# Two kinds of expert layer: gate weights spread over 128 rows, the gate's steps in other slots, first products ahead of the first gate weights

## The reference, cut to what matters

```
nx = rmsnorm(X) * g2                                   # per token, 128 values
rw = softmax(nx @ Wr.T + expert_bias)                  # 8 experts
topw, topi = top_k(rw, 2);  topw = softmax(topw)
combine = sum(one_hot(topi, 8) * topw)                 # 8 gate weights a token, 6 are zero
shared = (silu(xf @ sW1.T) * (xf @ sW3.T)) @ sW2.T     # for every token
eo[e]  = (silu(xf @ eW1[e].T) * (xf @ eW3[e].T)) @ eW2[e].T
X + shared + sum over e of combine[:, e] * eo[e]
```

## Time and profile before

| | us |
|---|---|
| median of 3 runs | 3324.93 (3316.59 to 3332.51) |
| the profiled execution, its own time | 3329.29 |
| its span in the profile | 3327.4 |
| mean granted TensorE clock | 0.904 of full speed |
| PE busy | 2785.1 (84%) |
| DVE busy | 2147.6 (65%) |
| POOL busy | 1693.1 (51%) |
| ACT busy | 1467.9 (44%) |

### The profile page before, as it was taken

How to read it: one execution, slowest core, us unless ns; L and a number is a source line. 1 busy time by engine, 2 the same in 40 slices (tenths; PEclk the granted TensorE clock), 3 DMA queues, 4 the chain that set the end, 5 groups by cost and what they waited for, 6 DMA issues and landing times. The chain is left out here.

```text
span 3327.4 us, 45520 instructions
## 1 busy us (share of the span) xinstructions
PE 2785.1 (84%) x13832; PEld 1834.1 (55%) x13832; DVE 2147.6 (65%) x4781; ACT 1467.9 (44%) x2308; POOL 1693.1 (51%) x1583
## 2 busy tenths in 40 slices
PE   3367896888569968878888887999799999979999
PEld 2245564566555546554444445667555555546666
DVE  5745673766557547665656656777477777767776
ACT  3433353545334535441111114555456666645555
POOL 5544654544136445534554544555566665545554
PEclk8688697989778969888999998999899999989999
DMA  1000110000001000010000001000000000010000
GB/s 31 0 11 2 45 36 22 1 1 1 15 23 39 21 22 1 1 50 1 1 1 0 0 0 39 1 1 1 10 1 1 1 0 1 1 39 4 7 7 10
DMA packets 36523, 37.19 MB, mean 11 GB/s; under 512 B 12536, under 2 KB 25208, under 8 KB 36088
## 3 DMA queue, kind: packets, MB, share of 16 engines
q1 hardware_dynamic: 36344, 34.95, 3.9%
HBM read 20.11 MB, written 2.10 MB: 7 GB/s over the span
## 5 line engine op out<-in xcount | busy, mean ns | idle before, releaser
L1757 DVE TENSOR_REDUCE l_diffneg_max<-psum 128x1 fp32r<-128x512 f32 x536 | 364.3, 688 | 124.9 <-PE psum L1510 119.5
L3547 POOL TENSOR_TENSOR l_moe1sc<-l_moe1s,l_moe1bcs 128x512 f32<-128x512 f32 x224 | 306.0, 1378 | 207.8 <-ACT l_moe1s L3271 201.1
L1677 ACT ACTIVATE l_diffweights<-psum 128x1024 f32<-128x1024 f32 x256 | 262.4, 1025 | 160.9 <-PE psum L1537 159.1
L3430 DVE TENSOR_TENSOR l_moe1g<-l_moe1sc,psum 128x512 f32<-128x512 f32 x256 | 174.4, 681 | 191.3 <-POOL l_moe1sc L3547 108.9
L3437 DVE TENSOR_TENSOR l_moe1g_lo<-l_moe1g,l_moe1g_hi 128x512 fp32r<-128x512 f32 x256 | 239.3, 936 | 0.0
L1510 PE MATMUL psum<-l_diffkz,l_diffQ 128*128 128x512 f32 x536 | 230.5, 431 | 0.3 <-DVE l_diffneg_max L1757 0.2
L373 PE MATMUL psum<-l_moe1h_hi,l_moe1w_hi 128*128 128x512 f32 x512 | 219.9, 430 | 7.0 <-DVE l_moe1g L3430 7.0
L148 POOL TENSOR_TENSOR settled<-powers 128x1 f32<-128x1 f32 x111 | 30.8, 277 | 365.4 <-DVE l_alibimv L207 106.3
L374 PE MATMUL psum<-l_moe1h_hi,l_moe1w_lo 128*128 128x512 f32 x512 | 205.3, 401 | 0.0
L375 PE MATMUL psum<-l_moe1h_lo,l_moe1w_hi 128*128 128x512 f32 x512 | 204.4, 399 | 0.0
L1088 DVE TENSOR_REDUCE l_attn0neg_max<-psum 128x1 fp32r<-128x512 f32 x256 | 167.2, 683 | 56.3 <-PE psum L831 53.6
(11 more groups left out here) (482 smaller groups left out, 7895.8 us busy)
## 6 DMA issues: line engine op xcount, KB each, us to landing
l_attn0Q<-l_attn0q_hi SPq DMA_DIRECT2D x128, 64.0 KB, 2.0
l_moe1w_raw<-in_moe_w SPq DMA_DIRECT2D x24, 256.0 KB, 5.6
l_attn0Q<-l_attn0q_lo SPq DMA_DIRECT2D x64, 64.0 KB, 2.0
l_moe0w_raw<-in_moe_w SPq DMA_DIRECT2D x24, 128.0 KB, 2.5
x<-in_x SPq DMA_DIRECT2D x8, 256.0 KB, 4.2
out<-x SPq DMA_DIRECT2D x8, 256.0 KB, 2.3
x<-in_light_w SPq DMA_DIRECT2D x3, 512.0 KB, 4.5
l_attn0Q<-l_attn0max_rows SPq DMA_DIRECT2D x64, 2.0 KB, 1.7
```

Of the source, the lines that this page charges most:

```text
L1677: nc.scalar.activation(weights[:, tt, 2 * pair:2 * pair + 2, :], ps[:, S[m % 2]:S[m % 2] + 2, :], ACT.Exp, scale=SCALE).then_inc(act_exp.s ...
L1757: nc.vector.tensor_reduce(neg_max[:, n % 2, st, row:row + 1], ps[:, bank_of(("max", n, b)), :], AXX, ALU.max, negate=True).then_inc(vec_ma ...
L3430: v.tensor_tensor(g[:, n % 2, h, :], (s if is_shared(n) else sc)[:, n % 2, h, :], ps[:, H3[(n * HT + h) % 3], :], ALU.mult).then_inc(vec_g ...
L3547: nc.gpsimd.tensor_tensor(sc[:, n % 2, h, :], s[:, n % 2, h, :], bcs[:, n % 2, :], ALU.mult).then_inc(pool_sc.sem, pool_sc.step("sc", h))
```

## The change

`hi` and `lo` of the eight gate columns go to a tile `gate` of 16 columns; the gate takes two matmuls of 16 columns a quarter instead of three of 8, and DVE adds the two halves with one more instruction. `comb`, `comb_rows` and `pick` get 128 rows, so the spreading product has 128 rows. In the first kind choice and e2 go to slot 4, weights to slot 5, the statistics to slot 3; `comb_turned` stays at slot 8. `out` goes behind the first silu of its slot. At the start of a block `up` of the first EARLY slots (2 and 1) stands ahead of `comb_turned(0)`, the second expert group and the statistics of sequence 1 ahead of the choice (first kind). Cut to its core:

```diff
         self.raw = sb("_raw", moe.cols)
         self.hi, self.lo = sb("_hi", moe.cols, F32R), sb("_lo", moe.cols, F32R)
         self.gain = sb("_gain", 1)
+        self.gate = sb("_gate", 16, F32R)
...
         if g < 0:
-            return [(slice(0, 8), True)]
+            return [(self.raw[:, 0:8], self.gate[:, 0:8], self.gate[:, 8:16], True)]
         moe = self.moe
...
-        at = lambda base: slice(base + a * moe.tiles * P, base + b * moe.tiles * P)
-        return [(at(moe.w1), True), (at(moe.w3), True), (at(moe.w2), False)]
+        of = [(slice(base + a * moe.tiles * P, base + b * moe.tiles * P), base != moe.w2) for base in (moe.w1, moe.w3, moe.w2)]
+        return [(self.raw[:, at], self.hi[:, at], self.lo[:, at], scaled) for at, scaled in of]
...
-            for span, _ in self.spans(g):
-                sp.dma_start(self.raw[:, span], self.core.dram[self.source][:, span]).then_inc(self.loaded[g], 16)
+            a, b = (min(e * self.AT_ONCE, self.moe.slots) * self.moe.tiles * P for e in (g, g + 1))
+            for base in (self.moe.w1, self.moe.w3, self.moe.w2):
+                at = slice(base + a, base + b)
+                sp.dma_start(self.raw[:, at], self.core.dram[self.source][:, at]).then_inc(self.loaded[g], 16)
...
     LO_ROW = 32
-    ROWS = LO_ROW + 8
     ps = core.psum
     real = lambda n: 0 <= n < N
     is_shared = lambda n: n % NE < moe.shared
     on_pool = lambda n: n % NE in ((1, 2, 5, 8) if moe.shared else (0, 2, 3, 4, 5, 6, 7))
+    EARLY = 2 if moe.shared else 1
     AT_TR, AT_GATE, AT_LO, AT_LOGITS = 0, 2 if moe.shared else 1, 1 if moe.shared else 0, 2 if moe.shared else 1
-    AT_CHOICE, AT_E2, AT_WEIGHTS, AT_COMB = (5, 6, 7, 8) if moe.shared else (2, 2, 3, 5)
-    AT_STATS, AT_SCALE, AT_Z = (4, 6, 7) if moe.shared else (4, 4, 5)
+    AT_CHOICE, AT_E2, AT_WEIGHTS, AT_COMB = (4, 4, 5, 8) if moe.shared else (2, 2, 3, 5)
+    AT_STATS, AT_SCALE, AT_Z = (3, 6, 7) if moe.shared else (4, 4, 5)
...
-        comb = sb("comb", [P, NQ, ROWS])
-        comb_rows = sb("comb_rows", [ROWS, 2, T], F32R)
-        pick = sb("pick", [ROWS, 8, P], F32R)
+        comb = sb("comb", [P, NQ, P])
+        comb_rows = sb("comb_rows", [P, 2, T], F32R)
+        pick = sb("pick", [P, 8, P], F32R)
...
-            u += [("tr", j + 1)] if e == AT_TR else []
+            u += [("comb", 0)] if n == EARLY - 1 else []
+            u += [("tr", j + 1)] if turns(n) else []
             u += [("gate", j + 1)] if e == AT_GATE else []
             u += [("comb", j + 1)] if e == AT_COMB else []
             return [x for x in u if 0 <= x[1] < NSEQ]
 
-        misc = [("tr", 0), ("gate", 0), ("comb", 0)] + [u for n in range(N + LAG + 1) for u in misc_users(n)]
+        turns = lambda n: n == EARLY - 1 if n < NE else n % NE == AT_TR
+
+        misc = [("tr", 0), ("gate", 0)] + [u for n in range(N + LAG + 1) for u in misc_users(n)]
...
                 misc_free(t, ("gate", j))
                 t.wait_ge(vec_lo.sem, vec_lo.done(j, "lo"))
                 for q in range(NQ):
-                    c = slice(q * P, (q + 1) * P)
-                    ins = product3(nc, ps[:, MISC, q * 8:q * 8 + 8], h_hi[:, j % 2, c], h_lo[:, j % 2, c], w_hi[:, 0:8], w_lo[:, 0:8])
+                    c, to = slice(q * P, (q + 1) * P), ps[:, MISC, q * 16:q * 16 + 16]
+                    nc.tensor.matmul(to, h_hi[:, j % 2, c], weights_in.gate[:, :], start=True, stop=False)
+                    ins = nc.tensor.matmul(to, h_lo[:, j % 2, c], weights_in.gate[:, :], start=False, stop=True)
                 ins.then_inc(pe_gate.sem, pe_gate.step("gate"))
...
@@ -3210,7 +3216,7 @@
                 misc_free(t, ("comb", j))
                 t.wait_ge(vec_gate.sem, vec_gate.done(j, "comb", 1))
                 for q in range(NQ):
-                    ins = nc.tensor.transpose(ps[0:ROWS, MISC, q * P:(q + 1) * P], comb[:, q, :], core.ident[:, :])
+                    ins = nc.tensor.transpose(ps[:, MISC, q * P:(q + 1) * P], comb[:, q, :], core.ident[:, :])
                 ins.then_inc(pe_comb.sem, pe_comb.step("comb"))
...
@@ -3218,20 +3224,19 @@
             gate(0)
             for n in range(N + LAG + 1):
                 j, e = divmod(n, NE)
-                if n == 0 and moe.shared:
-                    up(0)
-                    comb_turned(0)
-                elif n == 0:
-                    comb_turned(0)
-                if real(n) and not is_shared(n):
+                if EARLY <= n < N and not is_shared(n):
                     weight_rows(n)
-                if real(n) and not (n == 0 and moe.shared):
+                if real(n):
                     up(n)
                 if real(n - LAG):
                     down(n - LAG)
                 if e == LAG and 0 <= j - 1:
                     tail(j - 1)
-                if e == AT_TR and j + 1 < NSEQ:
+                if n == EARLY - 1:
+                    comb_turned(0)
+                    for m in range(moe.shared, EARLY):
+                        weight_rows(m)
+                if turns(n) and j + 1 < NSEQ:
                     head_turned(j + 1)
                 if e == AT_GATE and j + 1 < NSEQ:
                     gate(j + 1)
...
-                copy(comb_rows[:, j % 2, :], ps[0:ROWS, MISC, :]).then_inc(act_comb.sem, act_comb.step("hi"))
+                copy(comb_rows[:, j % 2, :], ps[:, MISC, :]).then_inc(act_comb.sem, act_comb.step("hi"))
...
             weights_in.scalar_group(a, 1)
             for n in range(N + LAG + 1):
                 j, e = divmod(n, NE)
-                if e == LAG and 0 <= j - 1:
+                if e == LAG and 0 <= j - 1 and not real(n):
                     out(j - 1)
-                if n == 0 and not moe.shared:
-                    comb_hi(0)
-                if real(n) and not is_shared(n):
+                if EARLY <= n < N and not is_shared(n):
                     weight_rows(n)
                 for h in range(HT):
                     if real(n):
                         silu(n, h)
+                    if h == 0 and e == LAG and 0 <= j - 1 and real(n):
+                        out(j - 1)
                     if real(n - 1):
                         product_hi(n - 1, h)
-                if n == 0 and moe.shared:
+                if n == EARLY - 1:
                     comb_hi(0)
+                    for m in range(moe.shared, EARLY):
+                        weight_rows(m)
                 if j == 0 and e % weights_in.AT_ONCE == 0 and 2 <= e // weights_in.AT_ONCE + 2 < weights_in.groups:
                     weights_in.scalar_group(a, e // weights_in.AT_ONCE + 2)
-                if e == AT_TR and j + 1 < NSEQ:
+                if turns(n) and j + 1 < NSEQ:
                     head_hi(j + 1)
                 if e == AT_COMB and j + 1 < NSEQ:
                     comb_hi(j + 1)
...
             def gate_logits(j):
                 vec_gate.start()
                 inc, wait = gate_steps(j)
-                found = ps[:, MISC, 0:NQ * 8].rearrange("p (q e) -> p q e", e=8)
+                found = ps[:, MISC, 0:NQ * 16].rearrange("p (q e) -> p q e", e=16)
+                of_hi, of_lo = found[:, :, 0:8], found[:, :, 8:16]
                 d.wait_ge(pe_gate.sem, pe_gate.done(j, "gate"))
                 d.wait_ge(vec_gate.sem, vec_gate.done(j, "comb", 1, back=1))
                 if bias is None:
-                    inc(v.tensor_copy(logits[:, :, :], found), "logits")
+                    inc(v.tensor_copy(ex[:, :, :], of_hi), "part")
+                    wait("part")
+                    inc(v.tensor_tensor(logits[:, :, :], ex[:, :, :], of_lo, ALU.add), "logits")
                 else:
-                    inc(v.tensor_tensor(logits[:, :, :], found, bias_sb[:, :].unsqueeze(1).to_broadcast([P, NQ, 8]), ALU.add), "logits")
+                    inc(v.tensor_tensor(hot1[:, :, :], of_hi, bias_sb[:, :].unsqueeze(1).to_broadcast([P, NQ, 8]), ALU.add), "part")
+                    wait("part")
+                    inc(v.tensor_tensor(logits[:, :, :], hot1[:, :, :], of_lo, ALU.add), "logits")
...
-                lo = comb_rows[LO_ROW:ROWS, j % 2, :]
-                v.tensor_tensor(lo, ps[LO_ROW:ROWS, MISC, :], lo, ALU.subtract).then_inc(vec_comb.sem, vec_comb.step("lo"))
...
-            ones_at = lambda c: core.ident[0:ROWS, c:c + 8].unsqueeze(2).to_broadcast([ROWS, 8, P])
+            ones_at = lambda c: core.ident[:, c:c + 8].unsqueeze(2).to_broadcast([P, 8, P])
...
                 d.wait_ge(bias_loaded, 16)
             gate_logits(0)
             weights_in.vector_group(d, 0)
+            if bias is not None:
+                weights_in.vector_group(d, 1)
+                statistics(1)
             gate_choice(0)
             gate_weights(0)
-            weights_in.vector_group(d, 1)
-            statistics(1)
+            if bias is None:
+                weights_in.vector_group(d, 1)
+                statistics(1)
             for n in range(N + LAG + 1):
                 j, e = divmod(n, NE)
                 if n == 0 and not moe.shared:
```

(19 more changed lines are left out.)

## The result

The changed kernel takes **3226.1 us** (median of 4 runs, 3225.6 to 3233.8) against 3325.8 for the kernel before (4 runs beside them): **ratio 0.9707, 95% interval 0.968 to 0.9735**, 2.9% faster. The forecast was 3205 with a range of 3138 to 3255. The profiled execution took 3225.6, 103.7 less than the one of before. First the head of its page, then the busy time of one block of either kind (as the earlier trace rows).

A forecast was written before the change was run, and what follows sets the result against it. PE was taken as busiest in the expert blocks, losing time at spreads, comb waits and starts, with a POOL and DVE chain beside it. Gains of 84 (first kind) and 38 (second) sum to 122: 3205 us, likelihood 0.65, range 3138 to 3255.

The forecast's parts named there:

- 128 rows, 0.39 each: Spreading product: at 128 rows its neighbours start 0.23 us apart, saving the whole 0.39 each time, 256 places.
- The rival in which padding brings nothing: Spreading product: the loss comes from its place, not its row count; 71 us gained in all, 3256; chance 0.07.
- Gate, 0.44 a gated turn: Gate products on PE: eight of 16 columns instead of twelve save 0.44 us a gated turn, about 0.85 at block starts.
- Second kind, turn 42.2: Steady turn, second kind: only savings in slots 0 to 2 count beside the POOL and DVE chain; 1.9 us off 44.1.
- Last sequence: Second kind's last sequence, without gate or chain: eight spreads at 0.39 save 3.1 us a block.
- First kind, turn 28.7: Steady turn, first kind: the 4.05 us wait for comb goes, shorter new waits come; 4.6 us saved of 33.3.
- The rival of the clock: First kind's turns: the clock stays low behind the new waits, returning about 25 us, 3232; chance 0.13.
- single waits: First-kind turn, from slot 3's start S: new PE waits of 0.7 for out, 1.5 and 1 to 3 for g_lo.
- First kind, last sequence: Last sequence of a first-kind block: spreads save 3.1 us, less 0.8 for out, so 2.3.
- Starts: Block start and first turn: 7.3 + 4.6 = 11.9 us saved in the first kind, 2.5 + 1.9 = 4.4 in the second.
- PE alone, 40.5 in the second kind: Both kinds: DVE and POOL keep up, turns of 24.2 and 40.5 us, 208 us gained, 3120; chance 0.13.
- The slower rival, POOL's slot 5 behind e2: First kind: POOL's slot 5 behind e2 holds slots 7 and 8; with 10 us, 19 slower, 3344; chance 0.02.

The follow-up runs named there:

- e7: The changed kernel with comb, comb_rows and pick back at 40 rows: 3282.8 us, ratio 0.9893 to the kernel before.
- e1: The kernel before with comb, comb_rows and pick at 128 rows, nothing else: 3275.3 us against 3322.4, ratio 0.9865.
- e11: The kernel before with 72 rows instead of 40 in the spreading product, one run: 3280.7 us against 3321.3.
- e12: The kernel before with only the gate as two 16-column products a quarter and one more DVE instruction: 3321.4 us against 3321.3, ratio 1.0.
- e10: The kernel before with 64 rows instead of 40 in the spreading product, one run: 3314.1 us against 3321.3.
- e8: The changed kernel with, in the second kind, e2 in slot 3, token scale and next tokens in slots 5 and 6: 3185.4 us, ratio 0.9592.
- e6: The changed kernel with the first kind's e2 in slot 5 instead of 4, behind POOL's scaling of slot 5: 3201.2 us, ratio 0.9641.
- e3: The kernel before with only the first kind's choice and e2 in slot 4, weights in 5, statistics in 3: 3304.1 us against 3322.4, ratio 0.9941.

## Why the forecast was right, and where its sizes were off

The direction, the range and the likeliest case held; the gain was 99.7 by the medians where 120 was forecast. Two slips in the forecast's range change nothing: 3138 lies four fifths, not half, of the way from 3205 to 3120, and turns of 27.7 to 30.5 with gains of 1.2 to 2.8 come to about 3178 to 3240. Step by step.

- **128 rows, 0.39 each: right in size, and e7 and e1 show it as the largest part** (57 us in the changed kernel; 47 alone, of which some 5 may be the clock's at the starts). The reason given, that a load is not pulled ahead where the row count changes, is wrong as put: from 128 to 72 rows and back it is pulled ahead (e11). What counts is whether the product has more than 64 rows; the forecast went to 128 and so did not depend on the difference. The rival in which padding brings nothing is out, and with it the rule of the Trainium skill that a single product with 32 rows takes the time of one with 128 (page "TensorE: Matmul & The Clock Gate", section "Why this matters for your kernels"), as a rule for a sum: the product itself is no longer, but going to 40 rows and back among 128-row products is.
- **Gate, 0.44 a gated turn: right on PE**, all of it reaches the end in the second kind (e12). At a block's start it saves 0.6, not 0.85. In the changed first kind no run parts it from the rest.
- **Second kind, turn 42.2: measured 42.6.** The working was right that the chain through POOL takes what PE saves behind slot 2; the share that counts was 1.5, not 1.9. Last sequence: 4.2 for 3.1, and the rows alone give 3.8 to 4.1 of it (e1, e7). The stretch behind the last turning of weights holds slots 6 and 7 of the sequence before as well, so ten spreads and not eight: 10 x 0.39 = 3.9. The forecast's seven turns and one sequence had left these two out.
- **First kind, turn 28.7: right at the full clock (28.4 to 29.0), wrong as a mean (29.9 and 29.3).** This is the term of the sum that was mis-sized. The forecast kept no low-clock product in the steady turns; 35 and 29 are left in the six turns of the two blocks, 64 x 0.19 = 12 us, about what these turns fell short of the forecast (43.4 gained, 54.8 forecast). The rival of the clock had the mechanism, with a chance of 0.13, and twice the size (25 us). The two were not alternatives: about half of what it priced came on top of the forecast.
- Inside that turn single waits were off both ways: `out` 0.6 (forecast 0.7); g_lo in slot 7 2.0 (1.5), since `ex` starts 0.5 later and takes 6.86, not 6.46, so that it ends at S + 8.8, not 8.1; g_lo in slot 8 0 to 0.5 (1 to 3), since `gate_weights` takes 1.1 (L3404 to L3417, 1240.58 to 1241.69) and is not held by POOL here; the rest of `comb` 1.1 to 1.45 (up to 0.4); h_lo ahead of the gate 0.54 (none). A sum of 28.9 from terms wrong by up to 1 us each is partly luck.
- **First kind, last sequence: 0.1 and 1.7 for 2.3.** The spreads there save 3.1, but in front of the first one PE waits 1.44 for `comb_rows`, which the forecast had at nothing. The first block's is the longer one (31.8 against 30.2): it has eight products at the lower clock, 8 x 0.19 = 1.5, the second has none. With e2 in slot 5 both have none and take 30.2.
- **Starts: 9.9 and 8.5 for 11.9; 3.8 and 2.4 for 4.4.** Slot 2 starts 6.8 earlier (forecast 7.3), so the first turn behind it gains 3.1 and 1.7 where 4.6 was booked: PE arrives early at slot 7 and waits 4.8 there for the chain through POOL, and the lower clock follows. In the second kind slot 1 starts 3.5 and 2.5 earlier (forecast 2.5) and the turn behind it gains nothing to speak of (forecast 1.9). I had booked a full turn's gain on top of the earlier start, as if the chain had no due time of its own. And up to 2.9 and 1.9 of the 9.9 and 8.5 may be the clock's, since 64 rows show that much with the old start (e10).
- **PE alone, 40.5 in the second kind: the rival's number was wrong.** It took 3.56 off the turn but left PE's waits of 1.6 in it; without them it is 38.9, and e8 has 38.5. With the right figure the room behind POOL's order was about 4 us a turn (42.6 less 38.5), and visible before.
- **The slower rival, POOL's slot 5 behind e2:** the order costs something (e6: 25 us), but far less than the rival needed; the forecast had it in its sum as the wait in slot 7.

**Open:** what lets the clock fall in the first kind. It fell behind waits of 1.4 in turns with 2 us of idle time in all (e3), and did not in turns with 4.15 that have a wait of 1.36 in the same place (e6); and the same code has turns of both sorts in one block (e1, e3, the changed kernel). No run held the waits and moved only their places.

## What to carry to other kernels

Look at the distances around any product with few rows between full ones: with 72 rows and more it cost nothing here, with 40 and 64 about 0.4 us in and out. Padding with zeros cost next to nothing: ACT's copy takes 0.59 us with 40 rows and 0.60 with 128, and POOL's clearing 0.3 us more, once a block. Move an engine's late-needed small steps (e2, and in the second kind the token scale and next tokens) behind the scaling that PE waits for, not ahead of it: by the medians this was worth 41 us in the second kind and 25 in the first. When a change removes one long wait and leaves several short ones, price the turn at both clock levels and book a share of each, and price the parts of a change together: alone they gave 70 of 100 us. When a part makes something start earlier, ask where the chain beside it is next due, and book no more than up to there.
